# A four-stage transformer kernel on one core: the near terms' stores and the position rows' transfers go to GpSimd's DMA queue

## The reference, cut to what matters

```python
scores = jnp.einsum('bhqd,bhkd->bhqk', q, k) / scale
rel = build_relative_position(S, S, BUCKETS, MAX_REL)      # log buckets of q - k, constant beyond about 64
c2p = jnp.take_along_axis(c2p_att, ...)                    # q times the position of bucket(q - k)
p2c = jnp.swapaxes(jnp.take_along_axis(p2c_att, ...), -1, -2)
scores = scores + (c2p + p2c) / scale
probs = jax.nn.softmax(scores, axis=-1)
ctx = jnp.einsum('bhqk,bhkd->bhqd', probs, v)
```

## Time and profile before

| | before |
|---|---|
| three timed runs | 749.48, 750.93, 753.38 us (median 750.93) |
| the profiled execution: its own time, its span | 750.15 us, 748.4 us |
| busy over the span: PE, DVE, ACT, POOL | 76%, 72%, 60%, 31% |
| granted TensorE clock, mean over the span | 0.884 of full |
| moved by DMA | 127.77 MB, mean 171 GB/s |
| DMA packets of SP's queue (q1), of POOL's queue (q0) | 116532 with 97.15 MB; 4704 with 27.88 MB |

### The profile page before, as it was taken

The page is one execution under the profiler, slowest core; times in us unless marked ns, Lnnn a source line. Parts: engine busy times, 40 slices in busy tenths (PEclk is TensorE's granted clock), DMA queues, the critical chain, the costliest instruction groups (busy, mean ns, idle before and its releaser), DMA issues. The chain is left out here.

```text
span 748.4 us, 17372 instructions
## 1 busy us (share of the span) xinstructions
PE 572.4 (76%) x5335; PEld 413.1 (55%) x5335; DVE 535.4 (72%) x1819; ACT 446.1 (60%) x961; POOL 229.7 (31%) x378
## 2 busy tenths in 40 slices
PE   4499892479898899999999997453995673688870
PEld 3398781146565566767667676342994342356440
DVE  7532437468786799999999994872224799867897
ACT  3244653257786688999899994650552534376723
POOL 5756442203491581274400000053443200211200
PEclk9999995578999899999999998555998797799995
DMA  9978598989997999999844412724553000000001
GB/s 241 255 255 267 188 277 246 213 203 245 268 353 299 268 343 363 241 287 351 224 137 116 126 53 78 188 83 142 185 167 104 3 0 0 1 1 1 0 1 57
DMA packets 125486, 127.77 MB, mean 171 GB/s; under 512 B 27572, under 2 KB 102468, under 8 KB 124500
## 3 DMA queue, kind: packets, MB, share of 16 engines
q1 hardware_dynamic: 116532, 97.15, 46.9%
q0 software_dynamic: 4704, 27.88, 9.8%
q10 hardware_dynamic: 4160, 1.63, 1.1%
HBM read 68.33 MB, written 48.75 MB: 156 GB/s over the span
## 5 line engine op out<-in xcount | busy, mean ns | idle before, releaser
L1721 DVE CUSTOM_DVE_ANT_0 l0am_prob<-l0am_ps_s,l0am_bias 128x512 f32<-128x512 f32 x256 | 163.1, 687 | 28.7 <-DMA l0am_bias<-near_terms 13.8
L1610 ACT ACTIVATE l0am_prob<-l0am_prob,l0am_neg_top 128x512 f32<-128x512 f32 x256 | 171.3, 722 | 11.2 <-DVE l0am_neg_top L1721 11.2
L1816 PEld LDWEIGHTS l0am_ps_t<-c_ident,l0am_prob 128*128 128x128 f32 x1024 | 113.5, 144 | 63.7 <-ACT l0am_prob L1610 42.2
L1816 PE MATMUL l0am_ps_t<-c_ident,l0am_prob 128*128 128x128 f32 x1024 | 137.0, 283 | 10.1 <-ACT l0o_rows L1289 6.7
L655 ACT ACTIVATE l0f_h<-l0f_psU,l0f_experts 128x128 f32<-128x128 f32 x212 | 60.4, 368 | 80.0 <-PE l0f_psU L979 78.9
L1803 PE MATMUL l0am_ps_s<-l0am_ks,l0am_qs 32*128 32x512 f32 x512 | 76.2, 666 | 19.6 <-DVE l0am_neg_top L1721 10.5
L1708 DVE COPY l0am_probT<-l0am_ps_t 128x1024 f32<-128x1024 f32 x64 | 78.2, 1221 | 3.0 <-PE l0am_ps_t L1816 2.5
L1604 ACT COPY l0am_probT<-l0am_ps_t 128x512 f32<-128x512 f32 x128 | 69.9, 589 | 15.9 <-PE l0am_ps_t L1816 10.3
L843 DVE COPY l0f_xsT<-l0f_psT 128x128 f32<-128x128 f32 x53 | 15.4, 290 | 87.2 <-PE l0f_psT L969 87.2
L545 POOL DMA_INDIRECT token_results<-l0f_ys,l0f_token_i x53 | 51.2, 967 | 71.8 <-DVE l0f_ys L853 67.8
L1425 POOL TENSOR_TENSOR l0am_near<-l0o_rows_q,l0o_rows_k 128x128 f32<-128x128 f32 (+4 forms) x192 | 67.9, 399 | 7.2 <-DMA l0o_rows_k<-position_k 6.7
(11 more groups left out here) (344 smaller groups left out, 936.3 us busy)
## 6 DMA issues: line engine op xcount, KB each, us to landing
l0am_bias<-near_terms SPq DMA_DIRECT2D x128, 192.0 KB, 4.6
near_terms<-l0am_near POOLq DMA_DIRECT2D x6, 3072.0 KB, 12.9
l0f_mine<-l0f_experts SPq DMA_DIRECT2D x53, 256.0 KB, 2.8
l0o_rows_k<-position_k SPq DMA_DIRECT2D x16, 512.0 KB, 6.5
near_terms<-l0am_near SPq DMA_DIRECT2D x4, 1536.0 KB, 9.0
l0f_experts<-in_L_ffn_w SPq DMA_DIRECT2D x2, 2048.0 KB
position_q<-l0o_rows SPq DMA_DIRECT2D x16, 256.0 KB, 8.2
position_k<-l0o_rows SPq DMA_DIRECT2D x16, 256.0 KB, 5.0
```

Source lines behind the costliest of these rows:

```text
L1610: nc.scalar.activation(prob[:, k, :], prob[:, k, :], ACT.Exp, bias=neg_top[:, k:k + 1], scale=-1.0)\
L1721: dve.tensor_tensor_reduce(out=prob[:, k, :], in0=ps_s[:, j, :], in1=bias[:, j, at:at + S], scale=-1.0, scalar=HUGE, op0=ALU.add, op1=ALU.min,
L1816: last = pe.transpose(ps_t[:, BANK_OF[j], i, :], prob[:, u % SLOTS_, i * P:(i + 1) * P], ident[:, :])
```

## The change

What it does, in four parts. Near stores: one (batch 0, group 0) stays on SP, all others are issued by POOL, by groups of heads, 32 partitions with 48 KB each. Rows of batches 1 to 3: their stores and loads are issued by POOL too, in program order between its near passes, with semaphores of their own (`late_out`, `late_in`). Near terms of batches 1 to 3: one pass of 64 queries in place of two of 32. Buffers: 8 row buffers in place of 6, and the turned input `xnT` keeps 2 batches in place of 4. `FAR_STEPS` of batches 2 and 3 come later (steps 22, 24, 36, 38 in place of 16, 18, 32, 34).

```diff
-FAR_STEPS = {5: (1, 0), 7: (1, 1), 16: (2, 0), 18: (2, 1), 32: (3, 0), 34: (3, 1)}
-ROW_STEPS = {...}
+FAR_STEPS = {5: (1, 0), 7: (1, 1), 22: (2, 0), 24: (2, 1), 36: (3, 0), 38: (3, 1)}
...
-    ROW_BUFS = 6
+    ROW_BUFS = BATCH_ROWS
...
+    def row_stored(self, engine, cn):
+
+        b, i = divmod(cn, BATCH_ROWS)
+        engine.wait_ge(*((self.late_out[i], 16 * b) if b else (self.rows_out[i], 16)))
...
         def near_stored(engine, b, g):
-            if b == 0:
-                engine.wait_ge(first_near_out[g], 16)
-            elif g == 0:
-                engine.wait_ge(near_out, 16 * len(LATER_PIECES) * b)
+            if b == 0 and g == 0:
+                engine.wait_ge(first_near_out, 16)
+            else:
+                engine.wait_ge(near_out[g], 16 * (b + 1 if g else b))
+
+        def store_near(queue, b, g, stored):
+
+            part, n = 64 * WIN, P // GROUPS
+            queue.dma_start(bass.AP(dram["near"].tensor, (b * P + g * n) * part, [(part, n), (1, part)]),
+                            near[g * n:(g + 1) * n, :]).then_inc(stored, 16)
...
             # SP
-                store_first_near(0)
+                store_near(sp, 0, 0, first_near_out)
...
-                store_first_near(1)
...
-                        if n == 1 and t < 2:
-                            store_first_near(2 + t)
-                        for kind, cn in LATE_STEPS.get(q, ()):
-                            if kind == "rows":
-                                opening.store_rows(sp, cn)
-                                opening.store_rows(sp, cn + 1)
...
-                        for later, pair, side in ROW_STEPS.get(q, ()):
...
-                            opening.load_rows(sp, later, pair, side)
...
             # POOL
+                def load_rows(b):
+
+                    for side in range(2):
+                        opening.wait_stored(pool, b, side)
+                        for pair in range(TABLE_CHUNKS):
+                            opening.load_rows(pool, b, pair, side)
+
+                for g in range(1, GROUPS):
+                    near_stored(pool, 0, g - 1)
+                    store_near(pool, 0, g, near_out[g])
+                    for cn in (range(BATCH_ROWS, BATCH_ROWS + QUARTERS), range(BATCH_ROWS + QUARTERS, 2 * BATCH_ROWS), ())[g - 1]:
+                        opening.store_rows(pool, cn)
+                pool.wait_ge(near_dve, 1)
+                load_rows(1)
                 pool.wait_ge(mean_ready, 2)
...
+                    for pair in range(TABLE_CHUNKS):
+                        rows_arrived(pool, b, pair)
+                        last = near_bands(pool, RUNS_OF[pair])
+                    last.then_inc(near_pool, 1)
+                    pool.wait_ge(near_pool, b)
+                    for g in range(GROUPS):
+                        store_near(pool, b, g, near_out[g])
+                    if b + 1 < B:
+                        for cn in range(BATCH_ROWS * (b + 1), BATCH_ROWS * (b + 2)):
+                            opening.store_rows(pool, cn)
+                        load_rows(b + 1)
+                    for g in range(GROUPS):
+                        near_stored(pool, b, g)
```

More of the change, by code:

```diff
@@ L1181, in __init__ @@
         self.rows_in = [sem(f"rows_in{k}") for k in range(TABLE_CHUNKS)]
+        self.late_out = [kept.enter_context(nc.semaphore(f"{name}_late_out{k}")) for k in range(self.ROW_BUFS)]
+        self.late_in = [kept.enter_context(nc.semaphore(f"{name}_late_in{k}")) for k in range(TABLE_CHUNKS)]
         self.gathered = [kept.enter_context(nc.semaphore(f"{name}_gathered{b}")) for b in range(B)]
@@ L1300, in copy_by_dve, with store_rows @@
         last.then_inc(self.rows_by_dve, 1)
-    def store_rows(self, sp, cn):
+    def store_rows(self, queue, cn):
         b, i = divmod(cn, BATCH_ROWS)
         side, quarter = divmod(i, QUARTERS)
-        sp.wait_ge((self.rows_by_act, self.rows_by_dve)[cn % 2], cn // 2 + 1)
-        sp.dma_start(bass.AP(self.dram["tab"][side].tensor, row_address(b, 0) + quarter * GROUP * S, [(HEADS * S, NP_), (S, GROUP), (1, S)]),
-                     self.rows[:, cn % self.ROW_BUFS, :]).then_inc(self.rows_out[cn % self.ROW_BUFS], 16)
+        queue.wait_ge((self.rows_by_act, self.rows_by_dve)[cn % 2], cn // 2 + 1)
+        queue.dma_start(bass.AP(self.dram["tab"][side].tensor, row_address(b, 0) + quarter * GROUP * S, [(HEADS * S, NP_), (S, GROUP), (1, S)]),
+                     self.rows[:, i, :]).then_inc((self.late_out if b else self.rows_out)[i], 16)
     def store_stack(self, sp, b, side):
@@ L1395, in relative_attend @@
         far_out, scaled, added = sem("far_out"), sem("scaled"), sem("added")
-        near_out = kept.enter_context(nc.semaphore(f"{name}_near_out"))
-        first_near_out = [sem(f"first_near_out{g}") for g in range(GROUPS)]
+        near_out = [kept.enter_context(nc.semaphore(f"{name}_near_out{g}")) for g in range(GROUPS)]
+        first_near_out = sem("first_near_out")
         near_cleared, near_corner = sem("near_cleared"), sem("near_corner")
@@ L1410, in view, with near_corners @@
             return bass.AP(t, offset, [(t.shape[1], P), *dims])
-        def near_corners(engine, q0=0, q1=64):
-            for a in range(q0, q1, 16):
+        def near_corners(engine):
+            for a in range(0, 64, 16):
                 c0 = a + 64 - RIGHT
@@ L1419, in near_corners, with near_bands @@
             return last
-        def near_bands(engine, runs, q0=0, q1=64):
+        def near_bands(engine, runs):
             for d0, d1, pq, _ in runs:
@@ L1442, in _ @@
             def _(sp):
-                def store_first_near(g):
-                    part = 64 * WIN
-                    sp.dma_start(bass.AP(dram["near"].tensor, g * (P // GROUPS) * part, [(part, P // GROUPS), (1, part)]),
-                                 near[g * (P // GROUPS):(g + 1) * (P // GROUPS), :]).then_inc(first_near_out[g], 16)
                 def store_far(b, part):
@@ L1530, in _ @@
             def _(pool):
-                def store_near(b, q0, q1):
-                    part = 64 * WIN
-                    own = [(part, P), (1, (q1 - q0) * WIN)]
-                    pool.dma_start(bass.AP(dram["near"].tensor, b * P * part + q0 * WIN, own),
-                                   bass.AP(near[:, :].tensor, q0 * WIN, own)).then_inc(near_out, 16)
                 for a in range(0, 64, 16):
```

40 lines of the change are left out of this document (13 added, 27 removed).

## The result

The changed kernel takes 813.59 us (median of 4 runs, 809.51 to 818.26), the kernel before 751.12 (4 runs): ratio 1.081, 95% interval 1.075 to 1.087. The profiled execution took 809.51 us, its span 807.8, with a mean granted clock of 0.858 (0.884 before).

The account below looks back on a forecast made before the run. The prediction took PE to bound the undisturbed attention, with late transfers disturbing it. From 750.15 us, gains of 17.7 and losses of 57.5, 6, 7.6 and 3 gave 806 us, range 780 to 822 for the likeliest case.

Parts of the forecast that it names:

- blocked loads: Likeliest case: near stores on POOL's queue hold up SP's bias loads; 806 us, range 780 to 822, chance 0.64.
- near stores by groups: Batches 1 to 3: each batch's four stores take 30.5 us and stall the bias loads, +57.5 us in all.
- lower bound of 48: Low end, in us, of the three bias stalls beside the later batches' near stores; the high end was 68.
- clock behind them: After each of the three stalls the granted clock falls, 2 us each: +6 us (0 to 6).
- row transfers: Row stores behind the near stores in POOL's queue share the engines with the held-up bias: +3 us.
- Step 0: First attention step: batch 0's group 1 store on POOL holds up SP's first bias loads, +7.6 us.
- Row buffers: Eight in place of six: batch 1's rows no longer wait for a store to free a buffer, -5.8 us.
- step 8: Its bias would no longer be late behind row loads in SP's queue: -3.4 us.
- One pass: Batch 1's near terms computed in 22 us in place of 29; step 16's wait and slow clock go, -6.5 and -2.
- POOL's issues: Direct row DMAs cost POOL about 1 us each to issue, 19 in some 20 us; nothing charged.
- The sum: All terms added to the profiled 750.15 us: -17.7 + 57.5 + 6 + 7.6 + 3 = 806.5 us.
- half block: Rival: near stores block half as long, 14.7 us a batch; 746 us, range 742 to 760, chance 0.14.

Follow-up runs that it names:

- e4: Kernel before, with only batches 1 to 3's near terms in one pass, stored from POOL in four DMAs of 32 partitions x 48 KB: 803.41 us, ratio 1.070.
- e1: Changed kernel, but each later batch's near terms leave in one store of 128 partitions x 48 KB: 767.13 us, ratio 1.020.
- e7: Changed kernel with batch 0's near stores of groups 1 to 3 back on SP's queue: 811.62 us, ratio 1.077.
- e5: Kernel before, with one near pass and four stores of 128 partitions x 12 KB for batches 1 to 3, rows on SP: 761.23 us, ratio 1.009.
- e6: Kernel before, with only the row transfers of batches 1 to 3 on POOL and eight row buffers: 753.43 us, ratio 1.000.
- e9: Kernel before, with one near pass, four stores of 128 partitions x 12 KB, eight row buffers, rows on SP: 761.25 us, ratio 1.011.

## Why the prediction was right

The forecast was 806 us, the likeliest case the blocked loads; it came to 813.59, and to 809.51 for the profiled execution, 2.4 of it ahead of the attention. By its steps:

- **The near stores by groups**, the term that decides: right in kind (e4 alone loses 51 us; e1 takes 46 us of the loss back by the shape of the stores alone), in the size of a block (30.5 us forecast, 30.7 to 30.8 measured) and in the sum: 57.5 us forecast, 57.5 by step starts. That the two agree so closely is partly luck. The waits for the bias are 17.93, 12.70 and 20.80 us, 51.4 in all, where 18.5, 18.5 and 20.5 were forecast; in the second batch a pause of PE's (below) and the low clock behind it make up the rest of the step. The waits stand at steps 14, 25 and 36, not 16, 26 and 38. The lower bound of 48 does not follow from the spare times that the prediction names, which give 46; nothing hangs on it.
- **The clock behind them**, +6, and **row transfers**, +3: about right as a sum, 7.7 in place of 9. Steps 14 to 24 take 3.6 us less where step 16's wait and its slow clock, 8.5 by the prediction, are gone, so they lose 4.9, and steps 25 to 35 lose 2.8. In these stand further waits for the bias, 2.10 us at step 18 and 1.82 at step 28, so the clock has less than 6. The +3 counted three batches, but batch 3 has no rows behind its stores: its step 36 starts 1.7 us behind the last large packet, steps 14 and 25 start 3.0 and 6.1 us behind theirs.
- **Step 0**, +7.6: 6.2 by its wait; the measured 8.7 holds the 2.4 from ahead of the attention. In all runs with batch 0's later stores on POOL whose traces are read step 0 waits 8.3 to 10.0 us, and with them on SP 3.0 to 3.4. But e7's median says that little of this is lasting: back on SP the same stores seem to cost nearly as much a few steps later. Where is not shown.
- **Row buffers**, -5.8, and **step 8**, -3.4: of the 9.2 us steps 0 to 8 gave 4.8. The wait for the row store is gone, and step 4 follows step 3 after 5.69 us in place of 12.55, which is 6.9 gained; the late bias at step 8 is still there, 3.56 us against 3.43 in the earlier trace rows, and from the start of step 6 to that of step 8 it takes 14.1 us in place of 12.0. The step that failed is step 8's: the row loads left SP's queue and went into POOL's, where they take turns with the bias on the same engines. The DMA view of 184 to 196 us after, and below it before:

```profile
q0 software_dynamic: 849, 2.97, 71.7%
q1 hardware_dynamic: 1023, 1.06, 28.8%
...
l0am_bias<-near_terms SPq DMA_DIRECT2D x7, 192.0 KB, 12.0
```

```profile
q1 hardware_dynamic: 4606, 2.78, 88.5%
...
l0am_bias<-near_terms SPq DMA_DIRECT2D x5, 192.0 KB, 4.8
```

  By the packet records 725 of the 849 are of 4,096 bytes and 0.19 us, the rest of 4 bytes; before, on SP's queue, the row loads' pieces are packets of 256 and 512 bytes. The pieces of a row load on POOL's queue thus travel as few large packets and get most of the engines' time. The bias then takes 12.0 us to land, in place of 4.8. The prediction had no term for row loads beside the bias of batch 0; its "row transfers" are the row stores behind the near stores.
- **One pass**: 22 us forecast, 23 measured. **POOL's issues**: about 1 us for a row load forecast, 0.9 measured (3.59 us for four); near stores 0.5. No wait of DVE or PE for the normalised tiles, with 0.9 us in hand where some 3 were counted (POOL ends them at 189.58, PE turns them at 190.45). POOL is no bound.
- **The sum** came out well because the gain that failed and the other misses were few microseconds beside the one large term.

On the rivals: the half block did not happen with groups of 32 partitions; e1, with 377 GB/s in its stores, comes nearest to it, 767 us, against the 742 to 760 that I gave it. In the stretches read here 49 KB packets let SP's through about one to one, the 4-byte packets counted.

The Trainium skill (DMA: Bandwidth & Descriptors, "Queues, rings and completion order") says that a DMA engine goes round the queues that have work and drains a whole packet of one before it turns to the next. The counts of 151 and 156 packets, 111 and 111, 831 and 807 agree.

## What to carry to other kernels

Before a transfer goes to a second queue, count packets: while both queues are full, a load here needed as many turns as it had packets per engine, and a turn lasted as long as the other queue's packet (3.7 us at 49 KB from 32 partitions, 1.9 from 128). The size of a packet is to be read from the trace and not from the program's pieces. A load that is due every step loses to a store of few large packets, and most to one that leaves 96 partitions unused. A store in two halves behind the two halves of its computation was worth more here than one pass with four stores at its end (e5); and a gain at one step has to be followed over the next steps before it is counted, since e6 and e9 gave theirs back there.

## What was not expected of the hardware

PE's own instructions seem to wait in the same turns. Three times inside the near stores' blocks PE stood still for over 1.8 us with nothing to wait for in the profile. Timeline of PE after, the longest, and the DMA view of 306 to 310 us:

```profile
309.92 3.36 PE L1822 MATMUL l0am_ps_t<-c_ident,l0am_prob 128*128 128x128 f32 x15 [4.18 <-issue]
```

```profile
q0 software_dynamic: 32, 0.79, 78.4%
q1 hardware_dynamic: 32, 0.02, 1.9%
q8 instruction: 1, 0.02, 1.5%
```

One packet of the instruction queue lies just ahead of PE's restart, beside one round of POOL's large packets: it ends at 308.65. The two others are 1.89 us at 235.39 and 3.23 us at 383.29; in the attention before there is none of over 0.8 us. e4 has three as well, of 2.18, 2.60 and 2.99 us. In all six a packet of the instruction queue ends 1.2 to 1.5 us ahead of the restart; such a packet comes about every 10 us of the attention in all three kernels, mostly without a pause. The Trainium skill (Runtime: NRT & Kernel Launch, "Instruction fetch mechanics") says that an engine fetches its instructions in 16 KiB blocks by DMA while it runs, and that this is mostly hidden. The packet of 0.02 MB, 16,384 bytes in the packet records, fits; if the pauses are such fetches, these are not hidden. Nothing shows which engine such a packet serves, and no run took this apart, so the cause is argued from the place of the rows and not shown.
